# The causal mask put into the attention banks by ACT instead of PE, with the order of work written anew

## The reference

```python
# part 1: conditioned attention, 16 heads of 16
xn  = rms_norm(x, g_norm) * (1.0 + scale) + shift        # scale, shift from cond @ W_emb
q, k, v = split_heads(xn @ W_qkv);  q, k = rms_norm(q, g_q), rms_norm(k, g_k)
o   = softmax(q @ k.T * d ** (-0.5)) @ v
r   = o + o @ W_out
# part 2: feed-forward with a second, causal attention that only modulates the gate
x2  = rms_norm(r, ln1_w)
scores = where(causal, (x2 @ Wq.T) @ (x2 @ Wk.T).T / sqrt(16), finfo.min)
attn   = softmax(scores) @ (x2 @ Wv.T) @ Wo.T
mod    = 0.1 * tanh(attn @ A)
h   = rms_norm(r, ln2_w)
gate_pre = h @ W_in.T + mod * (h @ A) @ B
out = x + r + (silu(gate_pre) * (h @ W_up.T)) @ W_down.T
```

## Time and profile before

| | |
|---|---|
| median of 3 runs | 746.01 us |
| the profiled execution's own time | 744.87 us |
| span of its profile, first to last instruction | 743.1 us |
| PE busy | 687.5 us, 93% |
| DVE, ACT, POOL busy | 63%, 44%, 29% |
| mean granted clock of PE | 0.954 |

### The profile page before, as it was taken

How to read it: one execution, slowest core, us unless ns; L and a number is a source line. 1 busy time by engine, 2 the same in 40 slices (tenths; PEclk the granted TensorE clock), 3 DMA queues, 4 the chain that set the end, 5 groups by cost and what they waited for, 6 DMA issues and landing times.

```text
span 743.1 us, 36384 instructions
## 1 busy us (share of the span) xinstructions
PE 687.5 (93%) x16224; PEld 626.3 (84%) x16224; DVE 469.8 (63%) x1058; ACT 327.4 (44%) x690; POOL 218.6 (29%) x197
## 2 busy tenths in 40 slices
PE   2456889999999999999999999999999999999897
PEld 2345788998999899998999889999989899998887
DVE  4457546667675766667685766667685756667442
ACT  3354335453544545453544545453544445353321
POOL 0211212414251432414241432414241422423032
PEclk9557689999999999999999999999999999999999
DMA  5133000010101001010101001010101000000000
GB/s 154 33 132 105 17 4 3 4 45 4 45 5 45 4 4 46 4 44 4 44 4 45 4 4 45 4 44 4 44 4 44 4 15 19 4 30 5 31 3 29
DMA packets 19725, 21.01 MB, mean 28 GB/s; under 512 B 3536, under 2 KB 18512, under 8 KB 19584
## 3 DMA queue, kind: packets, MB, share of 16 engines
q1 hardware_dynamic: 19584, 18.81, 8.3%
HBM read 14.61 MB, written 4.19 MB: 25 GB/s over the span
## 4 chain that ended last, share of the span: by engine, by line
PE 85%; DVE 6%; issue 3%; ACT 2%; POOL 1%; DMA 1%; SPq 1%; POOLq 0%; DVEq 0%; ACTq 0%
PE gate_bank L369 13%; PE down_bank L561 12%; PE up_bank L369 12%; PE x_bank L361 7%; PE a_banks L447 6%; PE b_banks L369 6%; PE a_banks L361 6%; PE b_banks L514 5%; PE b_banks L382 3%; PE b_banks L361 3%; PE a_banks L382 3%; PE a_banks L419 2%; PE gate_bank L547 2%; PE x_bank L396 1%; PE b_banks L497 1%
## 5 line engine op out<-in xcount | busy, mean ns | idle before, releaser
L967 POOL TENSOR_TENSOR gl<-gu,gh 128x512 fp32r<-128x512 f32 x64 | 82.5, 1290 | 40.4 <-ACT gh L716 40.4
L955 POOL TENSOR_TENSOR qk<-qk,rx 128x512 f32<-128x512 f32 x32 | 33.5, 1067 | 198.2 <-DVE rx L764 198.2
L854 DVE SCALAR_TENSOR_TENSOR th<-th,gate_bank 128x512 f32<-128x512 f32 x64 | 43.3, 676 | 75.1 <-ACT th L711 75.0
L369 PE MATMUL gate_bank<-uh,win_hi 128*128 128x256 f32 x256 | 78.7, 307 | 0.2
L561 PE MATMUL down_bank<-wdn_hi,gh 128*128 128x256 f32 x256 | 76.4, 298 | 1.0 <-POOL gl L967 0.7
L962 POOL TENSOR_TENSOR zb<-zb,rib 128x512 f32<-128x512 f32 x32 | 33.5, 1048 | 142.6 <-DVE rib L781 142.6
L369 PE MATMUL up_bank<-uh,wup_hi 128*128 128x256 f32 x256 | 74.8, 292 | 0.0
L369 PE MATMUL gate_bank<-ul,win_hi 128*128 128x256 f32 x256 | 72.4, 283 | 0.0
L369 PE MATMUL gate_bank<-uh,win_lo 128*128 128x256 f32 x256 | 72.3, 282 | 0.0
L561 PE MATMUL down_bank<-wdn_lo,gh 128*128 128x256 f32 x256 | 71.8, 280 | 0.0
L369 PE MATMUL up_bank<-ul,wup_hi 128*128 128x256 f32 x256 | 71.8, 280 | 0.0
(11 more groups left out here) (151 smaller groups left out, 1958.5 us busy)
## 6 DMA issues: line engine op xcount, KB each, us to landing
xa<-in_x SPq DMA_DIRECT2D x16, 256.0 KB, 3.1
xres<-in_x SPq DMA_DIRECT2D x16, 256.0 KB, 3.0
out<-outb SPq DMA_DIRECT2D x16, 256.0 KB, 2.2
stage<-in_w_inT SPq DMA_DIRECT2D x2, 512.0 KB, 4.1
stage<-in_w_upT SPq DMA_DIRECT2D x2, 512.0 KB, 3.5
stage<-in_w_downT SPq DMA_DIRECT2D x2, 512.0 KB, 3.7
stage<-in_w_qkv SPq DMA_DIRECT2D x2, 384.0 KB, 3.5
we<-in_w_emb SPq DMA_DIRECT2D x1, 512.0 KB, 4.7
```

The costliest lines, as they stand in the source:

```text
L369: mm = pe.matmul(dst, w[a][:, k, c0:c0 + P], mov[b][:, k, :], start=(first and k == 0 and j == 0), stop=(last and k == KT - 1 and j == 2), ...
L854: dve.scalar_tensor_tensor(out=whole, in0=whole, scalar=1.0, in1=Gb[:, :], op0=ALU.add, op1=ALU.mult).then_inc(f_half, 1)
L955: pool.tensor_tensor(heads_of, heads_of, rx[:, 32 * t:32 * t + 32].unsqueeze(2).to_broadcast([P, 2 * H, HD]), ALU.mult).then_inc(done[name ...
L967: pool.tensor_tensor(gl[:, c % 2], gu[:, c % 2], gh[:, c % 2].bitcast(F32), ALU.subtract).then_inc(f_lo, 1)
```

## The change

The two bf16 matmuls of `b_scores0` are gone, and with them the bf16 identity. Two new ACT steps, `b_mask0` and `b_mask1`, copy the mask into the first and the second of `b_banks`, each as soon as that bank has been read out. `b_scores0` waits for both, and all scores matmuls add to what stands in the banks. So that they add, the second half of `b_q` and of `b_k` no longer starts its bank anew (the new last argument `m == 0` of `feature_major`). ORDER is written anew from end to end, with some steps in other periods (`x_turn` now shift 2, `f_up0` and `b_pv0` to `b_pv3` now shift 0, `f_up3`, `f_down1` to `f_down3` now -1), and WEIGHTS_AT with it. The core of the diff:

```diff
 ORDER = [
-    ("b_k", 0), ("f_tanh2", -1), ("a_rms", 1), ("a_copy1", 1), ("b_q", 0), ("b_k_out0", 0), ("b_k_out1", 0),
+    ("b_mask0", 0), ("a_scale0", 1), ("a_turn1", 1), ("b_mask1", 0), ("f_tanh2", -1), ("b_scores0", 0),
...
 WEIGHTS_AT = [
-    (-1, "r_rms", 2), (-1, "r_hi", 3), (-1, "b_k_out1", 4), (-1, "b_v0", 5), (-1, "b_v0", "v2"),
-    (-1, "b_shift1", 6), (0, "a_rowsum0", 7), (0, "f_lo3", 8), (0, "a_pv2", 9), (0, "f_tanh1", 10),
+    (-1, "x_square", 2), (-1, "r_hi", 3), (-1, "b_v0", 4), (-1, "f_tanh2", 5), (-1, "f_tanh2", "v2"),
+    (-1, "b_v_out0", 6), (-1, "b_pv0", 7), (-1, "a_rowsum1", 8), (0, "x_shift", 9), (0, "f_half0", 10),
...
-                        mm = feature_major(Bb[:, i, m * BLOCK:(m + 1) * BLOCK], wqkv2, i * D + m * P, (uh[odd], ul[odd]))
+                        mm = feature_major(Bb[:, i, m * BLOCK:(m + 1) * BLOCK], wqkv2, i * D + m * P, (uh[odd], ul[odd]), m == 0)
...
-                        if isinstance(n, int) and n == 0:
-                            pe.wait_ge(prep, 3)
-                        for bank in range(2):
-                            pe.matmul(Bb[:, bank, :], identb[:, :], maskb[:, :, :].rearrange("p h s -> p (h s)"),
-                                      start=True, stop=False, skip_group_check=True)
+                        wait(pe, done["b_mask0"], n)
+                        wait(pe, done["b_mask1"], n)
...
+                elif name in ("b_mask0", "b_mask1"):
+                    i = int(name[-1])
+                    for out_step in (("b_q_out",), ("b_k_out0", "b_k_out1"))[i]:
+                        wait(act, done[out_step], n)
+                    if isinstance(n, int) and n == 0:
+                        act.wait_ge(prep, 3)
+                    act.activation(Bb[:, i, :], maskb[:, :, :].rearrange("p h s -> p (h s)"), ACT.Copy).then_inc(done[name], 1)
```

More of the change, by code:

```diff
@@ L98, in bass_adaln_attention_ffn @@
         ident = sb("ident", [P, P])
-        identb = sb("identb", [P, P], BF16)
         causal = sb("causal", [P, S])
```

12 lines of the change are left out of this document (4 added, 8 removed), and 24 rows, old and new, of the table ORDER.

## The result

The changed kernel took 756.93 us (756.67 to 759.27, 4 runs), the kernel before in the same job 745.97 us: a ratio of 1.0155, with a 95% interval of 1.0119 to 1.0190. Forecast were 739.0 us and a range of 732 to 744.5. The profiled execution has a span of 755.4 us, 12.3 more than before.

The account below looks back on a forecast made before the run. PE was taken to bound the middle, chains the fill and drain. -0.57 us per block over 14 blocks (-8.0), outer blocks -1.4, drain +1.9, fill +1.0 gave -6.5 us: 739.0 us predicted, range 732 to 744.5.

Parts of the forecast that it names:

- The mask: PE's stream at b_scores0: the slot of the two mask matmuls goes, -0.53 us per block.
- Sides of islands: PE's changes between whole-array and 32x32 work: 24 sides per period become 20, dearer turns set against it, -0.20 us per block.
- waits that go: PE's weight loads in the middle: waits for m_mul and the scaled q and k vanish, -0.22 us per block.
- Waits that come: Covers too thin: f_gate1 waits for f_half0 (0.20 us), r_turn for r_norm's chain (0.18), together +0.38 per block.
- The islands put together: a_pv0 with a_pv1, a_pv2 with a_pv3: 10 islands for 12, three further sides saved, -0.29 us before dearer turns.
- The middle as PE's stream: From 100 to 640 us PE is the bound to half a percent; only its stream and its waits count.
- The ends: Fill, drain and outer blocks: outer blocks -1.4 us, drain +1.9, fill +1.0 (between -3 and +4).
- C: Rival: exposed chains at upper ends, sides worth nothing, fill +4 eat the gain; 745 us, 750 if all combine; chance 0.17.
- Rival D: Slower: ACT's queue is late with b_q_out and copies for b_scores0; 753 us at 2 us delay; chance 0.07.

Follow-up runs that it names:

- mask_only: Kernel before, in its old order, with the masks copied on ACT and PE's mask matmuls gone: 751.41 us, ratio 1.0087 to the kernel before.

## Why the prediction was wrong

Per block in the middle the sum was -0.57 us; measured are +0.54 (slots of blocks 3 to 12, after less before). Step by step:

- **The mask**, -0.53: right. The slot is gone, and `b_scores0` waits for no copy in the middle. Cover forecast 4.2 us of PE's work, copies 0.60 each, measured 0.62.
- **Sides of islands and waits that go**, -0.20 and -0.22: right together, -0.44. The slots that lost a side are shorter as counted (`f_up0` 1.61 to 1.42, `b_v0` 0.93 to 0.74, `f_down0` 1.60 to 1.42, `m_turn` 0.35 to 0.18), `f_down3` gained two (1.42 to 1.61). `a_turn0`, now between two islands, takes 0.59 us for 0.36 to 0.41, about what two sides cost. `m_turn` behind an island takes 0.18 where it took 0.35 ahead of one, so a side is not charged alike everywhere, as the prediction had suspected.
- **Waits that come**, +0.38: half right. `r_turn`'s is there (0.13 for 0.18). `f_gate1`'s for `f_half0` isn't, since the two islands that cover it had become longer than I took them for.
- **The islands put together**: here the forecast failed first. The step says "now `a_pv0` with `a_pv1` and `a_pv2` with `a_pv3` stand together, which makes 10 islands and 20 sides", and prices it by the sides alone. But `a_pv1` waits for `a_pv0` and `a_pv3` for `a_pv2`, in the code and before too. Before, another step stood between and hid it; now the first island of a pair costs 0.91 us and not 0.68, twice per block, +0.46. The price of a pair was taken as twice the slot of an island that stood alone.
- **The middle as PE's stream**: "In the middle only what stands in PE's stream counts, and what makes PE wait". Here it failed a second time: what makes PE wait was looked for among the other engines alone. The supply of its instructions was in the profile (0.2 to 0.7 us waits by "issue" at islands before) and no rival had it. It is some +0.9 us per block against before, in the mean slots of blocks 3 to 12: `f_gate1` 0.44, `r_mm` 0.16, `f_gate3` 0.12, `a_scores1` 0.10, the rest at the `pv` islands. That PE stops there for its instructions is shown by where the gaps lie. Why it stops longer in this order is argued only: removing the masks and the sides made the dense stretch shorter for nearly the same instructions (3.66 us for 256, not 3.78), and putting islands in pairs made it uneven. The mean density alone does not order the kernels: mask_only lost 0.92 at 3.80.
- **The ends**: forecast +1.5 with the outer blocks, measured +3.5, of it 2.4 in the fill. The drain's two chains are as forecast: the last `f_gate1` waited 1.5 us for DVE's `th`, the last `r_turn` 2.7 for ACT's `tok` (1.4 before, and +1.4 was forecast). The piece at 1.2 GHz in the drain was not forecast.
- **The range** ended at 744.5 and C at 750 (its own terms sum to 750.5 from the profiled execution, 751.6 from the median). Both new terms were outside what the rivals could give, so the chances rested on a list that was not complete. Rival D's chance of a slower kernel was no hit: its mechanism did not occur.

The two missed terms, 0.46 + 0.9, less the 0.2 of `f_gate1`, are 1.1 us per block, 16 of the 18 us between 739.0 and 756.9; the fill is the rest. What remains open: why the losses grow from block to block at nearly the same place in after, and what makes a place good or bad.

## What to carry to other kernels

When a kernel is bound by an engine whose instructions are small, count its instructions per microsecond in each stretch beside its busy time: work taken out of a dense stretch, or small work gathered there, can be lost again to supply. A step that is moved away from between two dependent ones uncovers their wait even when both are on one engine. When gaps of PE get longer, look at its granted clock behind them: here a second loss stood there that the idle time does not show. And before an offload is dropped because it came with a slower order, try it in the old order with a cover: here that version was 0.8% faster than the kernel before.
